# Second attention layer, groups 2 to 6: the query projection by seven block products (Strassen-Winograd) in place of eight

## The chip, the cores and the metric

One core of one Trainium2 chip. The metric is the device time of one execution in microseconds (us), lower is better. PE is TensorE, DVE VectorE, ACT ScalarE, POOL GpSimd, SP SyncE.

## What is computed

`x` has 16 sequences of 64 tokens, so T = 1024 tokens of E = 512. Two layers follow each other, each an attention block and a feed-forward block, each added to `x` behind a layer norm with a gate. The change is in the second layer's attention: H = 32 query heads of D = 128 and 8 key heads, so that 4 query heads share a key head; queries and keys are normed (rms) over D.

```
q = _rmsnorm((h @ Wq.T) as 32 heads of 128, q_norm_w)      # h = layernorm(x), 1024 x 512
k = _rmsnorm((ctx @ Wk.T) as 8 heads, k_norm_w), repeated for the 4 query heads of a group
scores = q . k / sqrt(128) + mask ; probs = softmax(scores)
x = x + tanh(g_xattn[1]) * ((probs . v) as 1024 x 4096) @ Wo.T
```

## The kernel before, in words

Every engine has its own instruction stream, written out by hand; semaphores join them. The order on each engine is that of the code. Activations stand transposed in SBUF, `hT` as 4 blocks of 128 rows (E) by 1024 tokens. Each fp32 operand is kept as a high part rounded to `fp32r` and a low part (the difference), `hT_hi` and `hT_lo`, `wq_hi` and `wq_lo`; a product is three matmuls, high with high, low with high, high with low (`three`, L226 to L228). ACT makes each high part by a copy, POOL each low part by a subtraction (`wq_lo`, L743; `wo_lo`, L1310).

An attention layer goes over G = 8 groups g of J = 4 heads and two halves h of 512 tokens; u = 2g + h is a unit. A step (g, h) of PE holds, in this order: the scores of unit u-1 (16 matmuls, L978), its folded sums of squares (L953, or L963 in the first units), the values of unit u-2 (24 matmuls, L1005), the query projection of unit u (4 heads of 12 matmuls 128x128 by 512 tokens), and the output projection of unit u-2 (4 token tiles of 12 such matmuls, into `ps_b`). In the steps (0, *) and (1, *), which open the layer, heads of the projection and the other pieces stand in a slightly different order: in (1,0) three heads, then the values of unit 0, then the fourth head.

ACT squares a head's queries into `q_sq` and copies them to `qT`; both read the PSUM bank in which PE has put the head. There are two such banks, used in turn, so the projection of head 2 waits for ACT's copy of head 0, and head 3 for head 1. DVE adds rows 0 to 63 and 64 to 127 of the squares to each other (`fold_squares`, L1470), and the scores of the unit wait for the last of these folds (`q_fold`). DVE transposes the sums of squares to `r_t` (semaphore `ssq_t`, for which the next projection waits) and copies them in eight 32x16 pieces to `r_s` (L1457); ACT makes 1/rms of them (`r_q`). DVE transposes the scores out of PSUM (L1435), scales them by `r_q` (L1479), adds the mask (L791), takes maxima (L1490, L1485), POOL or DVE subtracts them (`att_shift`, L797), ACT takes the exponential (L1177), DVE sums (L1502), POOL divides (`att_normalise`, L803), DVE transposes to `pT` (L1512), ACT makes `p_hi` (L1184) and DVE `p_lo` (L808), for which the values wait. Of their result in PSUM ACT makes `o_hi` and DVE `o_lo` (L1518), for which the output projection waits; DVE adds its tiles to `x_sb` (L1529).

In the layer's opening ACT's `r_q` of unit u-1 stands ahead of the squares and copies of heads of unit u. In the loop, POOL waits for DVE's `r_s` copies ahead of the second `wo_lo` of a step (g, 0):

```
for j in wo if do_finish and h == 0 and not (isinstance(g, int) and g == 1) else ():
    if lay and j == 1:
        pool.wait_ge(*c("ssq_all", us + 1))
    wo_low(g - 1, j)
```

The feed-forward block of this layer has small adapters; `lora_center` (L2132) is POOL's one part of it within the attention. It is written in POOL's step (0,1), and its instruction, at 766.31, falls into PE's step (1,0).

## Time and profile before

| | us |
|---|---|
| median of 3 runs | 1179.5 (1179.32 to 1179.86) |
| profiled execution | 1179.01 |
| its span | 1177.1 |
| PE busy | 1169.5 (99% of the span) |
| DVE busy | 880.9 (75%) |
| POOL busy | 532.9 (45%) |
| ACT busy | 424.0 (36%) |

The span runs from the first to the last instruction that the profiler records; 1.9 us lie outside. The second attention layer lies between 746 and 1150 us, and the steps that the change calls woven, (2,0) to (6,1), between the starts of the scores at 814.01 and at 1074.74.

### The profile page before, as it was taken

Reading aid. Unit: us, or ns where it says so; the run is one execution under the profiler, and the core shown is the slowest. Engines: PE = TensorE matmul, PEld = TensorE weight load, DVE = VectorE, ACT = ScalarE, POOL = GpSimd, SP = SyncE. Lnnn points to the kernel's source line nnn. Section 1 sums busy time; section 2 is a strip of 40 time slices with the busy share of each in tenths; the row PEclk is TensorE's granted clock in tenths of the full one; section 3 lists DMA queues with packets and bytes.
Section 4 is the critical chain, followed back from the end, with each engine's and each line's share of the span. In section 5 each row is a group of like instructions: output and inputs, shape, how many; then the busy total and the mean of one; then the engine's idle time right before and its main releaser. Section 6 shows DMA issues by size and latency. Waiting matters only on the chain.

```text
span 1177.1 us, 17132 instructions
## 1 busy us (share of the span) xinstructions
PE 1169.5 (99%) x6272; PEld 946.7 (80%) x6272; DVE 880.9 (75%) x1538; ACT 424.0 (36%) x748; POOL 532.9 (45%) x371
## 2 busy tenths in 40 slices
PE   9999999999999999999999999999999999999998
PEld 8888888888788888777788888777777777777776
DVE  4656646898888888889984335798888887888695
ACT  5145152322322222231552123535453443435542
POOL 5522533766667676677463112305242433425410
PEclk9999999999999999999999999999999999999999
DMA  7944735812211221211210003121221221121101
GB/s 286 285 137 159 211 111 162 287 55 81 81 66 59 89 80 45 80 45 45 99 64 36 1 1 107 55 94 57 91 80 45 80 80 54 71 89 39 43 1 72
DMA packets 57315, 106.54 MB, mean 91 GB/s; under 512 B 3633, under 2 KB 36529, under 8 KB 51889
## 3 DMA queue, kind: packets, MB, share of 16 engines
q1 hardware_dynamic: 56736, 104.82, 26.0%
q0 software_dynamic: 384, 1.05, 0.2%
q8 instruction: 32, 0.52, 0.2%
q14 instruction: 19, 0.15, 0.0%
q10 hardware_dynamic: 144, 0.00, 0.0%
HBM read 78.59 MB, written 27.26 MB: 90 GB/s over the span
## 4 chain that ended last, share of the span: by engine, by line
PE 96%; DVE 2%; issue 0%; ACT 0%; DVEq 0%; POOL 0%; POOLq 0%
PE ps_q L226 14%; PE ps_b L226 14%; PE ps_b L228 14%; PE ps_b L227 14%; PE ps_q L227 13%; PE ps_q L228 13%; PE ps_s L978 5%; PE ps_b L1005 4%; PE ps_s L278 1%; PE ps_q L953 1%; PE ps_q L2152 1%; PE ps_b L479 1%; PE ps_s L1847 1%; PE ps_q L529 0%; PE ps_b L529 0%
## 5 line engine op out<-in xcount | busy, mean ns | idle before, releaser
L226 PE MATMUL ps_q<-hT_hi,wq_hi 128*128 128x512 f32 x512 | 203.2, 397 | 0.0
L227 PE MATMUL ps_q<-hT_lo,wq_hi 128*128 128x512 f32 x512 | 199.6, 390 | 0.0
L228 PE MATMUL ps_q<-hT_hi,wq_lo 128*128 128x512 f32 x512 | 199.2, 389 | 0.0
L226 PE MATMUL ps_b<-wo_hi,o_hi 128*128 128x512 f32 x440 | 171.6, 390 | 0.0
L227 PE MATMUL ps_b<-wo_lo,o_hi 128*128 128x512 f32 x440 | 171.2, 389 | 0.0
L228 PE MATMUL ps_b<-wo_hi,o_lo 128*128 128x512 f32 x440 | 171.2, 389 | 0.0
L743 POOL TENSOR_TENSOR wq_lo<-wq_raw,wq_hi 128x512 fp32r<-128x512 f32 x64 | 90.2, 1413 | 112.8 <-ACT wq_hi L737 112.8
L1317 POOL TENSOR_TENSOR qT<-q_t 128x512 f32<-128x512 f32 x64 | 89.8, 1405 | 66.3 <-DVE q_t L1430 60.8
L226 PEld LDWEIGHTS ps_q<-hT_hi,wq_hi 128*128 128x128 f32 x512 | 96.1, 188 | 24.3 <-issue 1.5
L228 PEld LDWEIGHTS ps_q<-hT_hi,wq_lo 128*128 128x128 f32 x512 | 96.1, 188 | 20.3
L227 PEld LDWEIGHTS ps_q<-hT_lo,wq_hi 128*128 128x128 f32 x512 | 96.2, 188 | 18.7
L1310 POOL TENSOR_TENSOR wo_lo<-wo_raw,wo_hi 128x512 fp32r<-128x512 f32 x56 | 83.5, 1507 | 56.4 <-ACT wo_hi L1142 38.3
L1184 ACT ACTIVATE p_hi<-pT 128x1024 fp32r<-128x1024 f32 x32 | 34.0, 1061 | 189.7 <-DVE pT L1512 189.7
L226 PEld LDWEIGHTS ps_b<-wo_hi,o_hi 128*128 128x128 f32 x440 | 82.6, 188 | 18.4 <-issue 1.4
L228 PEld LDWEIGHTS ps_b<-wo_hi,o_lo 128*128 128x128 f32 x440 | 82.6, 188 | 17.1
L227 PEld LDWEIGHTS ps_b<-wo_lo,o_hi 128*128 128x128 f32 x440 | 82.6, 188 | 17.1
L1529 DVE SCALAR_TENSOR_TENSOR x_sb<-ps_b,gates,x_sb 128x512 f32<-128x512 f32 x115 | 81.4, 722 | 18.0 <-PE ps_b L228 17.5
L803 POOL TENSOR_TENSOR p_sb<-p_sb,p_rec 128x1024 f32<-128x1024 f32 x29 | 55.7, 1920 | 83.8 <-DVE p_rec L1506 83.8
L1518 DVE TENSOR_TENSOR o_lo<-ps_b,o_hi 128x512 fp32r<-128x512 f32 x128 | 81.8, 682 | 12.6 <-ACT o_hi L1191 10.7
L1191 ACT ACTIVATE o_hi<-ps_b 128x512 fp32r<-128x512 f32 x128 | 66.5, 607 | 34.0 <-PE ps_b L1005 26.7
L1177 ACT ACTIVATE p_sb<-s_sb,zero_b 128x1024 f32<-128x1024 f32 x32 | 37.2, 1162 | 96.9 <-POOL s_sb L797 93.5
L797 POOL TENSOR_TENSOR s_sb<-s_sb,mx_c 128x1024 f32<-128x1024 f32 x28 | 53.8, 1921 | 32.1 <-DVE mx_c L1485 32.1
(301 smaller groups left out, 2498.0 us busy)
## 6 DMA issues: line engine op xcount, KB each, us to landing
wq_raw<-in_wq SPq DMA_DIRECT2D x16, 1024.0 KB, 4.8
wo_raw<-in_wo SPq DMA_DIRECT2D x16, 1024.0 KB, 4.8
kT<-kT_spill SPq DMA_DIRECT2D x32, 256.0 KB, 4.3
v_hi<-v_hi_spill SPq DMA_DIRECT2D x16, 512.0 KB, 3.7
v_lo<-v_lo_spill SPq DMA_DIRECT2D x16, 512.0 KB, 4.7
v_hi_spill<-vs_hi SPq DMA_DIRECT2D x12, 512.0 KB, 5.4
v_lo_spill<-vs_lo SPq DMA_DIRECT2D x12, 512.0 KB, 6.7
kw_raw<-in_wk SPq DMA_DIRECT2D x4, 1024.0 KB, 9.2
```

The source lines that it names most:

```text
L226: nc.tensor.matmul(dst, l_hi, r_hi, start=first, stop=False)
L227: nc.tensor.matmul(dst, l_hi, r_lo, start=False, stop=False)
L228: return nc.tensor.matmul(dst, l_lo, r_hi, start=False, stop=last)
L743: nc.gpsimd.tensor_tensor(wq_lo[:, :, j * D:(j + 1) * D], wq_raw[:, :, j * D:(j + 1) * D], wq_hi[:, :, j * D:(j + 1) * D].bitcast(F32), AL ...
L797: eng.tensor_tensor(sc, sc, wide(mx_c[:, :], QB), ALU.subtract).then_inc(c["s_shifted"], 1)
L803: eng.tensor_tensor(pr, pr, wide(p_rec[:, :], QB), ALU.mult).then_inc(c["p_normed"], 1)
L978: last = nc.tensor.matmul(ps_s[par * S:(par + 1) * S, t * JS:(t + 1) * JS], kT[:, h, b:b + S], qT[:, h, :, b:b + S], start=True, stop=True)
L1191: nc.scalar.activation(o_hi[:, 2 * half:2 * half + 2, :, par * S:(par + 1) * S], ps_b[n].rearrange("p (t j q) -> p t j q", t=2, j=J), ACT. ...
L1310: nc.gpsimd.tensor_tensor(lo, wo_raw[:, j, :], hi.bitcast(F32), ALU.subtract).then_inc(c["wo_lo"], 1)
L1317: nc.gpsimd.tensor_tensor(qT[:, h, j, :], q_t1[:, j % 2, :], q_t2[:, j % 2, :], ALU.add).then_inc(c["q_rot"], 1)
L1518: nc.vector.tensor_tensor(o_lo[part], ps_b[n].rearrange("p (t j q) -> p t j q", t=2, j=J), o_hi[part].bitcast(F32), ALU.subtract).then_inc ...
L1529: nc.vector.scalar_tensor_tensor(x_sb[:, i, :], out_bank(u, t)[:, :], gates[:, lay:lay + 1], x_sb[:, i, :], ALU.mult, ALU.add).then_inc(c[ ...
```

## The change

In the second layer's steps (2,0) to (6,1) the projection of one unit (512 rows of E by 4 heads of 128 by 512 tokens) is cut into 2 by 2 blocks in each of its three dimensions: rows of E (two of the four blocks of 128), heads (two of four, WD = 256 columns), tokens (QT = 256). Eight block products would be the plain form; Winograd's form of Strassen's algorithm takes seven, of sums of blocks, and adds the results up. Of one block product PE issues 12 matmuls 128x128 by 256 tokens (`product`), 84 in a unit in place of 48 by 512.

- Left operands: `wq_raw` blocks a11, a12, a22 and the sums s1 to s4. POOL makes the four sums (128x512) and all seven low parts once a group, ACT the seven high parts.
- Right operands: two token blocks of `hT` as they are, and the mixed sums t1 to t4 (128x1024, both halves at once) of `hT`'s high and low parts. They are made once: ten sums and four low parts on POOL, four high parts on ACT, in steps (0,1), (1,0) and (1,1), beside the first group's weight sums.
- Results: PSUM banks `ps_q` and `ps_h` collect products; ACT copies one part to `qT` and one to `q_sq`, DVE adds four times a bank and a part in SBUF (`joined`), POOL adds once (`c22_made`).
- In the woven steps ACT and not DVE copies the eight pieces to `r_s` (`sums_by_quadrant`), folds are two additions 64x1024 in place of four 64x512, and the wait for `ssq_all` ahead of the second `wo_lo` is not there.
- The weight of the query norm is no longer applied in the copy to `qT` but, times the key's, when keys are staged (`kT_st`). The layer's loop runs over g = 2 to 5, and g = 6 is written out.

On PE:

```diff
+        def woven(lay, g):
+            return lay == 1 and not (isinstance(g, int) and g in (0, 1, G - 1))
...
+        WOVEN_PARTS = ("a11", "s2", "s3", "a12", "a22", "s1", "s4")
...
+            def project_woven(g, h):
+                u = 2 * g + h
...
+                def product(bank, name, right, first, last_one=False):
+                    if h == 0:
+                        turn = 7 * (g - 2) + WOVEN_PARTS.index(name) + 1
+                        pe.wait_ge(*c("woven_hi", turn))
+                        pe.wait_ge(*c("woven_lo", turn))
...
+                    for q in range(2):
+                        for k in range(2):
+                            col = slice(q * D, (q + 1) * D)
+                            dst, closes = bank[:, q * QT:(q + 1) * QT], last_one and (q, k) == (1, 1)
+                            nc.tensor.matmul(dst, l_hi[:, k, col], r_hi[:, k, :], start=first and (q, k) == (0, 0), stop=False, skip_group_check=True)
+                            nc.tensor.matmul(dst, l_hi[:, k, col], r_lo[:, k, :], start=False, stop=False, skip_group_check=True)
+                            last = nc.tensor.matmul(dst, l_lo[:, k, col], r_hi[:, k, :], start=False, stop=closes, skip_group_check=True)
...
+                pe.wait_ge(*c("ssq_t", u))
+                if h == 0:
+                    pe.wait_ge(*c("t_hi", 4))
+                    pe.wait_ge(*c("t_lo", 4))
+                product(ps_q[0], "a11", tokens(0, 0), True).then_inc(c["product"], 1)
+                product(ps_q[1], "s2", mixed(t2_hi, t2_lo), True, True).then_inc(c["product"], 1)
+                pe.wait_ge(*c("s_turned", u))
+                product(ps_h[0], "s3", mixed(t3_hi, t3_lo), True).then_inc(c["product"], 1)
+                pe.wait_ge(*c("copied", 2 * n + 1))
+                product(ps_q[0], "a12", tokens(1, 0), False, True).then_inc(c["q_done"], 1)
+                product(ps_h[1], "s1", mixed(t1_hi, t1_lo), True).then_inc(c["q_done"], 1)
+                pe.wait_ge(*c("joined", 4 * n + 2))
+                product(ps_h[0], "a22", mixed(t4_hi, t4_lo), False, True).then_inc(c["q_done"], 1)
+                pe.wait_ge(*c("copied", 2 * n + 2))
+                product(ps_h[1], "s4", tokens(1, 1), False, True).then_inc(c["q_done"], 1)
```

On ACT: the woven step, and what is added to step (1,0):

```diff
+                sums_by_quadrant(us)
+                norms(us)
+                act.wait_ge(*c("product", 3 * n + 1))
...
+                nc.scalar.activation(qT[:, h, 0:2, late], heads(ps_q[0]), ACT.Copy).then_inc(c["copied"], 1)
+                out_high(up, 0)
+                out_high(up, 1)
+                if building:
+                    woven_high(act, g + 1, "a11")
+                out_high(up, 2)
+                out_high(up, 3)
+                if building:
+                    woven_high(act, g + 1, "s2")
+                act.wait_ge(*c("q_done", 4 * u + 1))
...
+                nc.scalar.activation(q_sq[:, 0:2, early], heads(ps_q[0]), ACT.Square).then_inc(c["q_sq"], 1)
+                nc.scalar.activation(qT[:, h, 0:2, early], heads(ps_q[0]), ACT.Copy).then_inc(c["q_rot"], J)
+                act.wait_ge(*c("q_done", 4 * u + 2))
+                nc.scalar.activation(q_sq[:, 2:4, late], heads(ps_h[1]), ACT.Copy).then_inc(c["copied"], 1)
+                if building:
+                    woven_high(act, g + 1, "s3")
+                exponentials(us)
+                act.wait_ge(*c("joined", 4 * n + 3))
+                square(slice(2, 4), early)
+                if building:
+                    woven_high(act, g + 1, "a12")
...
+                act.wait_ge(*c("joined", 4 * n + 4))
+                square(slice(0, 2), late)
+                act.wait_ge(*c("c22_made", n + 1))
+                square(slice(2, 4), late)
+                if building:
+                    woven_high(act, g + 1, "a22")
+                    woven_high(act, g + 1, "s1")
+                    woven_high(act, g + 1, "s4")
...
+                probs_high(us)
...
+                if second_opening(lay, g, h):
+                    mixed_high(t1_hi, t1_f, 3)
+                    mixed_high(t2_hi, t2_f, 8)
```

On POOL: the mixed sums, the woven step, steps (1,0) and (1,1), and the end of (0,1):

```diff
+            def mixed_first(f, t, l, r):
+                pool.wait_ge(*lns[2]("lo", NT))
+                nc.gpsimd.tensor_tensor(by_half(f), quarters(hT_hi, *l), quarters(hT_hi, *r), ALU.subtract).then_inc(c["t_f"], 1)
+                nc.gpsimd.tensor_tensor(by_half(t), quarters(hT_lo, *l), quarters(hT_lo, *r), ALU.subtract).then_inc(c["t_f"], 1)
+            def mixed_joined(f, t, turn):
+                pool.wait_ge(*c("t_f", turn - 1))
+                nc.gpsimd.tensor_tensor(f[:, :, :], f[:, :, :], t[:, :, :], ALU.add).then_inc(c["t_f"], 1)
+            def mixed_next(f, l, r, turn, before):
+                pool.wait_ge(*c("t_f", before))
+                nc.gpsimd.tensor_tensor(by_half(f), quarters(hT_hi, *l), by_half(r), ALU.subtract).then_inc(c["t_f"], 1)
+                pool.wait_ge(*c("t_f", turn - 1))
+                nc.gpsimd.tensor_tensor(by_half(f), by_half(f), quarters(hT_lo, *l), ALU.add).then_inc(c["t_f"], 1)
...
+            def woven_step(g, h, next_wq):
+                u = 2 * g + h
...
+                late = slice(QT, HALF)
+                if h == 0:
+                    for j in range(J):
+                        wo_low(g - 1, j)
+                elif building:
+                    woven_sum(pool, g + 1, "s2")
+                    woven_sum(pool, g + 1, "s3")
+                    woven_low(pool, g + 1, "a11")
+                att_shift(pool, lay, u - 1)
+                pool.wait_ge(*c("copied", 2 * n + 2))
+                pool.wait_ge(*c("joined", 4 * n + 2))
+                nc.gpsimd.tensor_tensor(qT[:, h, 2:4, late], qT[:, h, 2:4, late], q_sq[:, 2:4, late], ALU.add).then_inc(c["c22_made"], 1)
+                if h and building:
+                    woven_sum(pool, g + 1, "s4")
...
+                att_normalise(pool, lay, u - 1)
+                if h == 0 and not (isinstance(g, int) and g == G - 2):
+                    woven_sum_first(pool, g + 1)
+                elif building:
+                    for name in WOVEN_PARTS[1:]:
+                        woven_low(pool, g + 1, name)
...
             def step(g, h, do_project, do_score, do_finish, next_wq):
                 uq, us = 2 * g + h, 2 * g + h - 1
+                if woven(lay, g):
+                    woven_step(g, h, next_wq)
+                    return
+                if second_opening(lay, g, h):
+                    mixed_joined(t3_f, t3_t, 6)
+                    att_normalise(pool, lay, us)
+                    mixed_next(t2_f, (1, 1), t1_f, 8, 3)
+                    woven_sum_first(pool, 2)
+                    woven_sum(pool, 2, "s2")
+                    woven_sum(pool, 2, "s3")
+                    woven_sum(pool, 2, "s4")
+                    mixed_low(t1_lo, t1_hi, t1_f, 1)
+                    return
+                if builds_woven(lay, g, next_wq):
+                    mixed_next(t4_f, (1, 0), t2_f, 10, 8)
+                    att_shift(pool, lay, us)
+                    mixed_low(t2_lo, t2_hi, t2_f, 2)
+                    woven_low(pool, 2, "a11")
+                    woven_low(pool, 2, "s2")
+                    att_normalise(pool, lay, us)
+                    woven_low(pool, 2, "s3")
+                    woven_low(pool, 2, "a12")
+                    mixed_low(t3_lo, t3_hi, t3_f, 3)
+                    woven_low(pool, 2, "a22")
+                    woven_low(pool, 2, "s1")
+                    mixed_low(t4_lo, t4_hi, t4_f, 4)
+                    woven_low(pool, 2, "s4")
+                    return
...
                     lora_center(pool)
+                    mixed_first(t1_f, t1_t, (0, 1), (0, 0))
+                    mixed_joined(t1_f, t1_t, 3)
+                    mixed_first(t3_f, t3_t, (1, 1), (0, 1))
```

On DVE, the woven step:

```diff
+                turn_sums(us, 1 - h, True)
+                turn_scores(us, 1 - h)
+                scale_scores(us)
+                dve.wait_ge(*c("copied", 2 * n + 1))
+                dve.wait_ge(*c("product", 3 * n + 2))
+                joined(part_b, ps_q[1], part_b).then_inc(c["joined"], 1)
+                att_mask(dve, lay, us, 1 - h)
+                dve.wait_ge(*c("joined", 4 * n + 1))
+                dve.wait_ge(*c("product", 3 * n + 3))
+                joined(part_d, ps_h[0], part_b).then_inc(c["joined"], 1)
+                maxima(us)
+                out_low(up, 0)
+                out_low(up, 1)
+                dve.wait_ge(*c("q_done", 4 * u + 3))
+                joined(qT[:, h, 2:4, early], ps_h[0], part_b).then_inc(c["joined"], 1)
+                out_low(up, 2)
+                dve.wait_ge(*c("q_done", 4 * u + 4))
+                joined(part_b, ps_h[1], part_b).then_inc(c["joined"], 1)
+                out_low(up, 3)
+                sums(us)
+                add_output(up, h, 0)
+                fold_woven(u, 0)
+                turn_probs(us)
+                fold_woven(u, 1)
+                att_probs_low(dve, lay, us)
+                for t in range(1, PAIRS):
+                    add_output(up, h, t)
```

What stands in POOL's queue from the end of step (0,1) to the end of step (1,1), after the 128x272 addition of `lora_center`. Before (L803 `att_normalise`, L743 `wq_lo` of the next group, L797 `att_shift`):

```order
L743 TENSOR_TENSOR wq_lo<-wq_raw,wq_hi 128x4x128 x4
L2132 TENSOR_TENSOR a_raw<-a_raw,a_mean 128x272
L803 TENSOR_TENSOR p_sb<-p_sb,p_rec 128x1024
L743 TENSOR_TENSOR wq_lo<-wq_raw,wq_hi 128x4x128
L797 TENSOR_TENSOR s_sb<-s_sb,mx_c 128x1024
L743 TENSOR_TENSOR wq_lo<-wq_raw,wq_hi 128x4x128 x2
L803 TENSOR_TENSOR p_sb<-p_sb,p_rec 128x1024
```

And of the change (L1562 to L1573 the mixed sums, L918 `att_normalise`, L827 and L848 the weight sums):

```order
L2498 TENSOR_TENSOR a_raw<-a_raw,a_mean 128x272
L1562 TENSOR_TENSOR t_f<-hT_hi 128x1024
L1563 TENSOR_TENSOR t_t<-hT_lo 128x1024
L1567 TENSOR_TENSOR t_f<-t_f,t_t 128x1024
L1562 TENSOR_TENSOR t_f<-hT_hi 128x1024
L1563 TENSOR_TENSOR t_t<-hT_lo 128x1024
L1567 TENSOR_TENSOR t_f<-t_f,t_t 128x1024
L918 TENSOR_TENSOR p_sb<-p_sb,p_rec 128x1024
L1571 TENSOR_TENSOR t_f<-hT_hi,t_f 128x1024
L1573 TENSOR_TENSOR t_f<-t_f,hT_lo 128x1024
L827 TENSOR_TENSOR wq_raw<-wq_raw 128x2x256
L848 TENSOR_TENSOR s_f<-wq_raw 128x512
```

Six additions of 128x1024 now stand between `lora_center` and the division of unit 1, and two (t2) between that and the first weight sum; the rest of t2 to t4, the sums and the low parts follow in step (1,1).

ACT's queue at the end of step (1,0), of the change (L1342 the exponential of unit 1, L1419 the high parts of t1 and t2, L1349 `p_hi` of unit 1, L1325 and L1327 `r_q` of unit 2; before, `p_hi` followed the exponential at once):

```order
L1342 ACTIVATE p_sb<-s_sb,zero_b 128x1024
L1419 ACTIVATE t_hi<-t_f 128x1024 x2
L1349 ACTIVATE p_hi<-pT 128x1024
L1325 ACTIVATE r_q<-r_s,eps_rms 128x32
L1327 ACTIVATE r_q<-r_q,zero_b 128x32
```

`p_hi` of unit 1 now stands behind the high part of t2, which waits for POOL.

DVE's queue in a woven step (g, 0). Before:

```order
L1444 STREAM_TRANSPOSE r_t<-ps_q 128x256
L1445 STREAM_TRANSPOSE r_t<-ps_q 128x256
L1457 COPY r_s<-r_t 32x16 x8
L1435 STREAM_TRANSPOSE s_sb<-ps_s 128x1024
L1479 TENSOR_TENSOR s_sb<-s_sb,r_q 128x1024
L791 TENSOR_TENSOR s_sb<-s_sb,mask_sb 128x1024
L1490 TENSOR_REDUCE mx_a<-s_sb 128x32
L1485 TENSOR_TENSOR mx_c<-mx_a 32x32 x4
L1518 TENSOR_TENSOR o_lo<-ps_b,o_hi 128x8x64 x4
```

And of the change (L1868 `joined`, the bank first):

```order
L1765 STREAM_TRANSPOSE r_t<-ps_q 128x256
L1766 STREAM_TRANSPOSE r_t<-ps_q 128x256
L1756 STREAM_TRANSPOSE s_sb<-ps_s 128x1024
L1807 TENSOR_TENSOR s_sb<-s_sb,r_q 128x1024
L1868 TENSOR_TENSOR qT<-ps_q,qT 128x2x256
L906 TENSOR_TENSOR s_sb<-s_sb,mask_sb 128x1024
L1868 TENSOR_TENSOR qT<-ps_s,qT 128x2x256
L1818 TENSOR_REDUCE mx_a<-s_sb 128x32
L1813 TENSOR_TENSOR mx_c<-mx_a 32x32 x4
```

The eight copies are gone from DVE, and two additions out of PSUM (there called `ps_s`, the bank is that of `ps_h`) stand ahead of the maxima; the other two stand between the four `o_lo`.

## Rows read from the trace of the kernel before

**Rows 1.** The page: span, busy times, shares of the chain
```profile
span 1177.1 us, 17132 instructions
PE 1169.5 (99%) x6272; PEld 946.7 (80%) x6272; DVE 880.9 (75%) x1538; ACT 424.0 (36%) x748; POOL 532.9 (45%) x371
...
PE 96%; DVE 2%; issue 0%; ACT 0%; DVEq 0%; POOL 0%; POOLq 0%
```

**Rows 2.** Chain that ended last (start, length, what): scores of steps (1,1), (2,0), (7,0)
```profile
787.71 1.95 PE ps_s L978 x16
...
814.01 1.88 PE ps_s L978 x16
...
1074.74 1.88 PE ps_s L978 x16
```

**Rows 3.** Busy time by engine over the ten steps
```profile
core 0: us, PE busy (x) PEld busy (x) DVE busy (x) ACT busy (x) POOL busy (x), PEclk, DMA share, GB/s
814.00:1075.00 261.00, 261.00 (x1525) 206.90 (x1526) 214.71 (x381) 113.86 (x201) 99.53 (x60) 1.00 0.19 67
```

**Rows 4.** Timeline of PE: start, length, line, tiles; projection, then values
```profile
899.78 0.39 PE L226 MATMUL ps_q<-hT_hi,wq_hi 128*128 128x512 f32 x1
900.01 0.39 PE L227 MATMUL ps_q<-hT_lo,wq_hi 128*128 128x512 f32 x1
...
921.05 0.28 PE L1005 MATMUL ps_b<-p_hi,v_lo 64*128 64x256 f32 x2
921.16 0.28 PE L1005 MATMUL ps_b<-p_hi,v_hi 64*128 64x256 f32 x2
```

**Rows 5.** Timeline of PE's weight loads, adapters' projection
```profile
1152.35 1.86 PEld L2152 LDWEIGHTS ps_q<-a_raw,xT 128*128 128x128 f32 x16
```

**Rows 6.** Timeline of DVE and POOL around masks, idle and beside POOL
```profile
847.55 1.23 DVE L791 TENSOR_TENSOR s_sb<-s_sb,mask_sb 128x1024 f32<-128x1024 f32 x1
...
871.23 1.29 POOL L1310 TENSOR_TENSOR wo_lo<-wo_raw,wo_hi 128x512 fp32r<-128x512 f32 x1 [3.04 <-DVE r_s L1457]
873.71 2.20 DVE L791 TENSOR_TENSOR s_sb<-s_sb,mask_sb 128x1024 f32<-128x1024 f32 x1
872.48 4.60 POOL L1310 TENSOR_TENSOR wo_lo<-wo_raw,wo_hi 128x512 fp32r<-128x512 f32 x2
```

**Rows 7.** Groups of instructions of POOL, 128x1024; and one such by timeline
```profile
L803 POOL TENSOR_TENSOR p_sb<-p_sb,p_rec 128x1024 f32<-128x1024 f32 x29 | 55.7, 1920 | 83.8 <-DVE p_rec L1506 83.8
...
422.73 2.40 POOL L808 TENSOR_TENSOR p_lo<-pT,p_hi 128x1024 fp32r<-128x1024 f32 x1 [1.28 <-ACT p_hi L1184]
```

**Rows 8.** Timeline of DVE, POOL and PE, first half of step (1,0)
```profile
765.71 1.95 DVE L1457 COPY r_s<-r_t 32x16 f32<-32x16 f32 x8
766.26 0.17 DVE L1457 COPY r_s<-r_t 32x16 f32<-32x16 f32 x1
766.44 0.67 DVE L1457 COPY r_s<-r_t 32x16 f32<-32x16 f32 x1
766.31 0.77 POOL L2132 TENSOR_TENSOR a_raw<-a_raw,a_mean 128x272 f32<-128x272 f32 x1 [3.65 <-ACT a_mean L2127]
767.69 1.23 DVE L808 TENSOR_TENSOR p_lo<-pT,p_hi 128x1024 fp32r<-128x1024 f32 x1
771.44 1.22 DVE L791 TENSOR_TENSOR s_sb<-s_sb,mask_sb 128x1024 f32<-128x1024 f32 x1
771.52 0.38 PE L1005 MATMUL ps_b<-p_hi,v_hi 64*128 64x256 f32 x2
```

**Rows 9.** One line's instructions, DVE: o_lo, first input in PSUM
```profile
L1518 DVE TENSOR_TENSOR o_lo<-ps_b,o_hi x128: 628/680/694, 228.5 to 1148.0; 128x512 fp32r<-128x512 f32 x128
```

**Rows 10.** Timeline of DVE and ACT, end of step (1,0)
```profile
786.20 1.41 DVE L1470 TENSOR_TENSOR q_sq<-q_sq 64x512 f32<-64x512 f32 x2
786.20 1.06 ACT L1184 ACTIVATE p_hi<-pT 128x1024 fp32r<-128x1024 f32 x1 [7.21 <-DVE pT L1512]
```

**Rows 11.** Timeline of ACT, last step: sums of squares
```profile
1121.19 1.90 ACT L1171 ACTIVATE r_s<-r_t 32x16 f32<-32x16 f32 x8 [3.32 <-DVE r_t L1447]
```

More of the change, by code:

```diff
@@ L19 @@
 JS = J * S
+QT = HALF // 2
+WD = 2 * D
 SC = PAIRS * JS
@@ new lines, in woven_parts @@
+        def woven_parts(name):
+            rows, cols = {"a11": (0, 0), "a12": (1, 0), "s1": (0, 1), "a22": (1, 1)}.get(name, (0, 0))
+            own = (slice(None), slice(2 * rows, 2 * rows + 2), slice(cols * WD, (cols + 1) * WD))
+            if name == "s2":
+                return s2_f[:, :, :], s2_hi[:, :, :], s2_lo[:, :, :]
+            if name == "s3":
+                return s3_f[:, :, :], s3_hi[:, :, :], s3_lo[:, :, :]
+            if name == "s4":
+                return s4_f[:, :, :], s4_hi[:, :, :], s4_lo[:, :, :]
+            return wq_raw[own], wq_hi[own], wq_lo[own]
```

229 lines of the change are left out of this document (193 added, 36 removed).

## The prediction

> **What bounds the kernel now.** The page comes first: PE is busy for 99% of a span of 1177.1 us and has 96% of the chain that ended last [rows 1]. So matmul time that goes comes off the end, and any wait that reaches PE is added to it. Second the chain: the scores of steps (2,0) and (7,0) start at 814.01 and 1074.74 [rows 2], ten steps in 260.7 us, 26.07 each, with no wait between. Third, what the other engines could take there: over those ten steps DVE is busy for 214.7 us of 261, ACT for 113.9, POOL for 99.5 [rows 3]. DVE has 4.6 us a step left, part of it bound to waits; on POOL much is free. Last, the room in the opening: PE's scores of step (1,1) start at 787.71 [rows 2]; the fourth fold of unit 2, for which they wait, ends at 786.20 + 1.41 = 787.61 [rows 10]. There is none.
>
> **What PE saves.** Projection matmuls of 512 tokens follow each other at 900.01 - 899.78 = 0.227 us; those with 256 columns, which go in pairs of rows, at 921.16 - 921.05 = 0.11 to 0.12 a pair [rows 4], 0.12 over a longer stretch. 128-column weight loads, one for each matmul, run at 1.86/16 = 0.116 [rows 5], just under that. I take 0.12: a unit has 48 x 0.2267 = 10.88 before and 84 x 0.12 = 10.08 after, 0.80 less, and ten units 8.0 less. At 0.116 it would be 11.4, at 0.125, 3.8: bounds for the pace.
> The Trainium skill, page "TensorE: Matmul & The Clock Gate", section "Back-to-back issue gap", gives a sustained pace of 81 ns at N = 128 and 131 ns at N = 512. Taken as a line between them, 256 columns would cost 98 ns, three quarters of 512 and not half, and by the ratio 84 x 98 against 48 x 131 the unit's 10.88 would become 14.2, ten units 33 us more. The rows have 227 ns where the page has 131, so I keep the rows.
>
> **What DVE and POOL do to each other.** A mask addition takes 1.23 us with POOL idle, and 2.20 when POOL has two `wo_lo` in hand; those two take 4.60, while one alone takes 1.29 [rows 6]. Two of 1.29 and two DVE additions (scale and mask) of 1.2 make 5.0, about that stretch. So they take turns, whole instruction by whole instruction, and the turn passes after each. It holds for small copies too: in `r_s`, one copy takes 0.17, the next, issued while POOL's 0.77 us addition runs, 0.67, until that ends [rows 8]. DVE instructions with an input in PSUM are free of it: 128 `o_lo` take 628 to 694 ns, whatever POOL does [rows 9]. Where POOL has one instruction now and then this costs nothing. The change puts rows of them there.
> A POOL addition of 128x1024 takes 1.92 with a broadcast input and 2.40 with two full ones [rows 7]. The mixed sums have two full ones: 2.40; the other end is 1.92.
>
> **The opening, step by step.** I follow every instruction from its queue and its semaphores, with the durations above and the turns; this is called the walk below. Before: POOL's `lora_center` ends at 767.08, the eight `r_s` copies at 767.66, `p_lo` of unit 0 runs 767.69 to 768.9, the mask from 771.44, and PE's values of unit 0 start at 771.52 [rows 8]. After: behind `lora_center` six additions of 2.40 follow at once. The fifth copy is the one held until 767.1; the last three wait for one addition each and are through at 769.5, 771.9 and 774.3, `p_lo` waits for the fourth, starts at 776.65 and ends at 777.7 (1.23, less 0.15 that a waiting instruction gains on its start). Values start at 777.8: **+6.3**. Scale and mask get their turns at 780.0 and 783.4, `o_lo` behind them ends at 785.8, where PE without it is ready at 782.0: **+3.8**. The second pair of `o_lo` gives **+0.45**. The division of unit 1 then ends at 796.0, DVE's transposition at 797.3, and the two last folds wait for t2's additions (2.40 each): 801.8, the scores of (1,1) start **+4.5** late. ACT's high part of t2 waits for t2 as well, and `p_hi` of unit 1, which ran at 786.20 [rows 10], stands behind it: values of unit 1 **+1.1**, sums' transposition +0.4. In (1,1) the `r_s` copies of unit 2 take turns with the low part of t1 and t4's two additions (3 x 2.40), and ACT's `r_q`, queued ahead of the squares of unit 3, holds the bank that head 2 needs: **+4.75**. The folds of unit 3 stand behind the division and five low parts: **+4.4**. Sum 25.7; the same walk of the kernel before gives 1.3 too much at the scores of (1,1), leaving 24.4. Then the first woven product waits for the low part of t4, +1.6, and one output for `o_lo`, +0.3. **Opening: +26.3.** The mechanism is robust in sign, since there is no room at 787.71, not in size: with 1.92 us in place of 2.40 the walk gives 6.8 less.
>
> **The woven steps.** DVE loses eight copies (1.4 us), gets four joins, each like `o_lo` 0.68, 2.7 us, and its four folds become two (1.41 for two of 512 [rows 10], so 1.1 for each of 1024, 0.6 less in all): about +0.7 a unit. ACT gets the eight copies at 1.90/8 = 0.24 us [rows 11], about as many copies and squares as it had, and is half idle: nothing by itself, but `r_q` comes some 0.5 later. POOL gets per group four sums, seven low parts for four, two additions to part C22: 9 x 1.29 = 11.6 us in 52. It has the time. But six low parts in a row now stand where DVE has its second fold and `p_lo`, and four `wo_lo` without the wait that had kept them behind the `r_s` copies (the "3.04 <-DVE r_s" of [rows 6]) stand at scale and mask. The walk gives, once per group in (g,0): scores 0.2 late for the fold, the first product 0.8 for the transposed sums queued behind `p_lo`, the product with a22 0.4 for the join that is queued behind the mask, the output 0.4 for `o_lo`: 1.8 for each of the four groups 3 to 6, **+7.2**. If DVE's and POOL's instructions fall otherwise, it is between 0 and 12. Of the new waits, POOL's for `joined` ahead of the C22 addition has the division and the low parts of the next group behind it, but the subtraction of the maxima ahead of it ends later than the join does; PE's for ACT's two copies of products end two products before they are asked for. SP's load of the next `wq_raw` waits for the seventh low part, some 20 us before its first use. The weight's factor, the removed increments, the moved small DMA and the written-out loop pass cost nothing I can find: they take instructions from engines that wait, hidden behind PE.
>
> **Sum.** -8.0 + 26.3 + 7.2 = +25.5 on 1179.0, the profiled execution (its span plus 1.9), 1204.5; the median of the runs is 0.5 above it. The 2.40 is the upper of its two prices, so I go slightly under: **1204**.
>
> **Rivals.** *A, the above,* 0.58: 1204, of its own 1196 to 1211 (the 1.92, 1198, the woven bounds, and clock: where PE stands for 4 to 6 us its granted clock could fall for a time, which no stretch here shows). *B, small copies keep their turn,* 0.15: the eight `r_s` copies wait once, not each, as if the 0.67 had been the only one that is ever held. The walk without them gives +15.2: 1194. For it: only one copy is seen held. Against: there was only one POOL instruction to hold them. The Trainium skill, page "SBUF — State Buffer", section "SBUF: two separate sides", has the port pair of these two engines as an exclusive lock, which whoever starts first keeps for its whole instruction, and names fp32 copies from SBUF to SBUF among those that take it; by that rule B's 1194 falls to A's 1204, and the held copy agrees. *C, the opening costs half of that or less and the woven steps give back what PE saves,* 0.08: 1181.5 to 1188. *D, the change's aim, faster,* 0.14: POOL's and DVE's instructions hardly hold each other (the 2.20 is a slow mask for another reason, as when the POOL input is what counts). The walk with no turns at all leaves 3.9 of stalls (`p_hi` of unit 1 behind t2, t4's low part) against 8.0: 1175. It decides from the point where opening and woven steps together lose less than 5.6 us, a sixth of the 33.5 that I have. Against it are the copies' 0.67 and the 4.60. *No difference,* 0.03. *E, small matmuls cost more than half,* 0.02: if each took the 946.7/6272 = 0.151 us that a weight load lasts in the mean of the whole run [rows 1], a unit would have 84 x 0.151 = 12.7, 1.8 more than before, ten 18: 1204.5 + 8 + 18 = 1231, or 1197 were the rest free. The pace in [rows 4, 5] speaks against it. By the figures of the Trainium skill above it would be 1246.
>
> **Range and chances.** A measurement of this kernel tells 0.2%, 2.4 us, from no change. Slower A + B + C + E = 0.83, same 0.03, faster 0.14. The range 1184 to 1212 leaves out D, the same, most of E and a part of C and of A's upper end, 2 in 10. A clock drop, or B with 1.92, stays within.
>
> **What would show it.** In the profile after: `r_s` copies of unit 1 with a mean over 1 us from 765.7 on, idle PE before values at about 777.8, before `ps_b` output, scores of (1,1) near 802, of (2,0) at about 838; `joined` near 0.7 us; ten woven steps in 260.7 - 8 + 9 = 261 to 262 us; block products at 0.12 us. Wrong if copies are not stretched, if the mixed sums run well under 1.9 us, if 256-column matmuls keep another pace, or if ten woven steps show less than 254 or over 268 us.

## The result and the profile after

The changed kernel takes 1203.57 us (median of 6 runs, 1203.34 to 1203.84) against 1179.41 for the kernel before, measured beside it (6 runs, 1178.95 to 1179.86): ratio 1.0205, interval 1.0192 to 1.0218. It is slower by 24.2 us. The profiled execution took 1203.78.

The page of the changed kernel (span; busy times; shares of the chain that ended last), against [rows 1]:

```profile
span 1202.0 us, 18025 instructions
PE 1170.3 (97%) x6632; PEld 960.7 (80%) x6632; DVE 930.4 (77%) x1478; ACT 446.6 (37%) x837; POOL 649.7 (54%) x430
...
PE 22%; DVE 10%; issue 3%; POOL 0%; DVEq 0%; ACT 0%
```

The span grew by 24.9 us, and PE is busy for 0.8 us more, with less to do. Both halves of that need an explanation: idle time that was not there before, and work that ran slower. The share of PE in the chain fell from 96% to 22%; the listed shares no longer add up, so the end is followed here on PE itself.

PE's timeline, the instructions of the opening with an idle time before them, and the scores of (7,0); the rows with L1138 are the scores of (1,1), (2,0) and (7,0), against [rows 2]:

```profile
775.55 0.39 PE L1165 MATMUL ps_b<-p_hi,v_hi 64*128 64x256 f32 x2 [3.70 <-issue]
...
783.40 0.47 PE L252 MATMUL ps_b<-wo_hi,o_hi 128*128 128x512 f32 x1 [1.67 <-issue]
...
789.40 0.47 PE L252 MATMUL ps_b<-wo_hi,o_hi 128*128 128x512 f32 x1 [0.28 <-DVE o_lo L1846]
...
799.31 3.68 PE L1138 MATMUL ps_s<-qT,kT 128*64 128x256 f32 x16 [4.21 <-issue]
804.23 0.39 PE L1165 MATMUL ps_b<-p_hi,v_hi 64*128 64x256 f32 x2 [0.21 <-DVE x_sb L1857]
...
814.61 0.80 PE L252 MATMUL ps_q<-hT_hi,wq_hi 128*128 128x512 f32 x1 [3.02 <-ACT qT L1318]
...
835.88 3.68 PE L1138 MATMUL ps_s<-qT,kT 128*64 128x256 f32 x16 [3.27 <-DVE q_sq L1791]
...
1097.86 1.95 PE L1138 MATMUL ps_s<-qT,kT 128*64 128x256 f32 x16
```

The scores of (1,1) come 11.6 us later than before and those of (2,0) 21.9. From (2,0) on little is added: (7,0) starts 262.0 us behind it, where ten steps took 260.7, and its values then wait 1.5. So nearly all of the loss arises in (1,0) and (1,1), as forecast. The two stretches of 16 scores at 3.68 us in place of 1.95 and 1.88 are the slower work.

Up to (2,0) there are seven idle times, 16.4 us in all, at places that the walk named; before, the same steps had 0.7, ahead of the scores of (1,1). What stands on the other side is in the timelines of DVE and POOL, first half of (1,0), against [rows 8], and in two rows of DVE from (1,1): the `r_s` copies of unit 2 and the last two folds of unit 3.

```profile
765.87 6.29 DVE L1778 COPY r_s<-r_t 32x16 f32<-32x16 f32 x8
772.19 3.26 DVE L923 TENSOR_TENSOR p_lo<-pT,p_hi 128x1024 fp32r<-128x1024 f32 x1
...
778.81 3.29 DVE L906 TENSOR_TENSOR s_sb<-s_sb,mask_sb 128x1024 f32<-128x1024 f32 x1
...
804.94 7.94 DVE L1778 COPY r_s<-r_t 32x16 f32<-32x16 f32 x8
...
831.13 4.52 DVE L1791 TENSOR_TENSOR q_sq<-q_sq 64x512 f32<-64x512 f32 x2
...
767.20 2.39 POOL L1562 TENSOR_TENSOR t_f<-hT_hi 128x1024 f32<-128x1024 f32 x1
...
772.02 2.34 POOL L1567 TENSOR_TENSOR t_f<-t_f,t_t 128x1024 f32<-128x1024 f32 x1
774.33 3.36 POOL L1562 TENSOR_TENSOR t_f<-hT_hi 128x1024 f32<-128x1024 f32 x1
```

Eight copies take 6.29 us in place of 1.95, `p_lo` 3.26 in place of 1.23, and the fourth POOL addition 3.36 in place of 2.39: each waits for the other engine's instruction in hand. In (1,1) the eight copies of unit 2 take 7.94, and the two folds that the scores of (2,0) wait for 4.52, where two took 1.41 [rows 10].

The slower work shows in windows. The columns are those of [rows 3]; the third number from the right is the granted clock as a share of 2.4 GHz:

```profile
775.50:789.00 13.50, 11.78 (x60) 9.28 (x60) 13.15 (x15) 5.35 (x8) 8.74 (x3) 0.87 0.00 1
799.30:803.00 3.70, 3.69 (x24) 2.00 (x32) 2.20 (x2) 1.40 (x2) 3.54 (x3) 0.50 0.02 4
...
815.00:820.00 5.00, 5.00 (x18) 3.96 (x18) 4.83 (x9) 2.48 (x6) 1.11 (x1) 0.75 0.00 0
836.00:840.00 4.00, 4.00 (x32) 1.82 (x32) 3.17 (x3) 0.00 (x0) 4.00 (x3) 0.50 0.00 0
840.00:845.00 5.00, 5.00 (x60) 4.34 (x45) 2.65 (x4) 3.12 (x12) 5.00 (x5) 0.86 0.23 66
845.00:1097.00 252.00, 245.05 (x1803) 211.14 (x1802) 231.25 (x313) 126.55 (x267) 162.76 (x97) 1.00 0.20 72
```

Each of the four idle times of 3.0 to 4.2 us lies in or ahead of such a stretch; 0.50 is the lower level, 1.2 GHz, for the whole of it. Length times what is missing from 1.00 is 1.76 + 1.85 + 1.25 + 2.00 + 0.70 = 7.6 us in the first five rows, some 8 with the stretches between them. The account at the scores of (2,1), 23.6 late (863.7 for 840.1), agrees: 0.3 by which the scores of (1,0) were late already, 15.7 of idle time more than before (16.4 less 0.7), less the 0.8 that the first woven unit saves, leave 8.4 for the clock by difference.

### The profile page after: what moved, and what is told of

The parts are those of the page before. It is cut to its first block and busy times, and to the rows that moved or that the text cites. A ratio compares the mean times of both kernels' runs of the same rounds, so it can differ in the third digit from the quotient of the medians.

```text
span 1202.0 us, 18025 instructions
## 1 busy us (share of the span) xinstructions
PE 1170.3 (97%) x6632; PEld 960.7 (80%) x6632; DVE 930.4 (77%) x1478; ACT 446.6 (37%) x837; POOL 649.7 (54%) x430
## 5 line engine op out<-in xcount | busy, mean ns | idle before, releaser
L252 PE MATMUL ps_q<-hT_hi,wq_hi 128*128 128x512 f32 x352 | 141.2, 401 | 3.0 <-ACT qT L1318 3.0
L253 PE MATMUL ps_q<-hT_lo,wq_hi 128*128 128x512 f32 x352 | 138.2, 393 | 0.0
L254 PE MATMUL ps_q<-hT_hi,wq_lo 128*128 128x512 f32 x352 | 137.8, 392 | 0.0
L1349 ACT ACTIVATE p_hi<-pT 128x1024 fp32r<-128x1024 f32 x32 | 33.9, 1061 | 171.7 <-DVE pT L1840 171.7
L918 POOL TENSOR_TENSOR p_sb<-p_sb,p_rec 128x1024 f32<-128x1024 f32 x29 | 55.6, 1918 | 62.8 <-DVE p_rec L1834 62.8
L252 PEld LDWEIGHTS ps_q<-hT_hi,wq_hi 128*128 128x128 f32 x352 | 66.7, 190 | 21.0 <-ACT qT L1318 3.4
L1342 ACT ACTIVATE p_sb<-s_sb,zero_b 128x1024 f32<-128x1024 f32 x32 | 37.0, 1156 | 120.1 <-POOL s_sb L912 113.7
L254 PEld LDWEIGHTS ps_q<-hT_hi,wq_lo 128*128 128x128 f32 x352 | 66.7, 189 | 14.4
L253 PEld LDWEIGHTS ps_q<-hT_lo,wq_hi 128*128 128x128 f32 x352 | 66.8, 190 | 12.9
L854 POOL TENSOR_TENSOR wq_lo<-wq_raw,wq_hi 128x512 fp32r<-128x512 f32 x44 | 66.1, 1511 | 18.7 <-ACT wq_hi L768 18.7
```

What stands on the lines that cost most here:

```text
L252: nc.tensor.matmul(dst, l_hi, r_hi, start=first, stop=False)
L253: nc.tensor.matmul(dst, l_hi, r_lo, start=False, stop=False)
L254: return nc.tensor.matmul(dst, l_lo, r_hi, start=False, stop=last)
L854: nc.gpsimd.tensor_tensor(wq_lo[:, :, j * D:(j + 1) * D], wq_raw[:, :, j * D:(j + 1) * D], wq_hi[:, :, j * D:(j + 1) * D].bitcast(F32), AL ...
L918: eng.tensor_tensor(pr, pr, wide(p_rec[:, :], QB), ALU.mult).then_inc(c["p_normed"], 1)
L1342: nc.scalar.activation(p_sb[:, :], s_sb[:, :], ACT.Exp, bias=zero_b[:, 0:1], scale=1.0 if lay else Q_SCALE).then_inc(c["p_exp"], 1)
```

## The experiments

The theory (A of the prediction): DVE and POOL take turns in the SBUF, whole instruction by whole instruction, and each idle time of PE also costs clock behind it. Its rivals: another part of the change makes the waits (the DVE joins, the removed wait, the moved copies), or the seven products themselves cost as much as eight.

**The long additions alone, in the kernel before.** Six additions of the size of the mixed sums, into a buffer that nobody reads there:

```diff
                     lora_center(pool)
+                    pool.wait_ge(*lns[2]("lo", NT))
+                    for n in range(6):
+                        if n:
+                            pool.wait_ge(lora["beside"], n)
+                        nc.gpsimd.tensor_tensor(ln_buf[:, :, :], hT_hi[:, 0:2, 0:E].bitcast(F32), hT_hi[:, 2:4, 0:E].bitcast(F32), ALU.subtract).then_inc(lora["beside"], 1)
```

> The kernel before, and behind lora_center on POOL six additions of 128x1024 of which nothing is used. Theory (DVE instructions with SBUF operands and POOL's instructions take turns): each of the last r_s copies and p_lo of unit 0 is held for one addition of 2.4, values of unit 0 start 4 to 6.5 late, the output projection another 1.5 to 4: 1185 to 1190. Rival (the delay comes from the order of the queues, p_hi behind the high part of t2, the division behind the sums): nothing here waits for the additions, 1179.4 within 0.5.

Measured: 1187.59, ratio 1.0073 (1.0057 to 1.009). The timeline of DVE, POOL and PE:

```profile
765.59 6.22 DVE L1462 COPY r_s<-r_t 32x16 f32<-32x16 f32 x8
766.92 17.46 POOL L1355 TENSOR_TENSOR ln_buf<-hT_hi 128x1024 f32<-128x1024 f32 x6
...
773.17 0.39 PE L1005 MATMUL ps_b<-p_hi,v_hi 64*128 64x256 f32 x2 [1.69 <-issue]
781.02 0.76 PE L226 MATMUL ps_b<-wo_hi,o_hi 128*128 128x512 f32 x1 [3.22 <-issue]
```

and the window behind the second wait:

```profile
781.00:785.00 4.00, 3.98 (x10) 3.13 (x11) 3.92 (x5) 0.00 (x0) 3.30 (x2) 0.50 0.00 0
```

The additions alone, with nothing else of the change, give the stretched copies, two new idle times on PE and the half clock behind the longer one. The wait ahead of the scores of (1,1) also grows, from 0.7 to 1.3. That is 8.4 us (1179.15 for the kernel before, measured beside it) out of six additions that no engine waits for: 5.5 of idle time more than before, and some 2.8 of clock.

**The same with memsets**, which write but read nothing (the edit against the run above):

```diff
-                        nc.gpsimd.tensor_tensor(ln_buf[:, :, :], ..., ALU.subtract).then_inc(lora["beside"], 1)
+                        nc.gpsimd.memset(ln_buf[:, :, :], 0.0).then_inc(lora["beside"], 1)
```

> The kernel before with six POOL instructions behind lora_center that write 128x1024 zeros and read nothing. Theory of turns for every POOL instruction: values of unit 0 late as with the additions, 1183 to 1188 if one takes 1 to 2.4 us. Rival (only POOL instructions that read SBUF hold DVE): 1178.9 to 1179.9.

Measured: 1180.80, ratio 1.0011 (1.0 to 1.0021), between the two ranges, so neither theory fits as it stands. The timeline says why:

```profile
766.11 5.33 DVE L1462 COPY r_s<-r_t 32x16 f32<-32x16 f32 x8
771.47 1.23 DVE L808 TENSOR_TENSOR p_lo<-pT,p_hi 128x1024 fp32r<-128x1024 f32 x1
...
767.42 6.02 POOL L1355 MEMSET ln_buf<- 128x1024 f32 x6
```

A memset takes 0.95 us. The copies are held by it (5.33 us for eight), but `p_lo`, with two inputs from the SBUF, runs its free 1.23 from 771.47 on while the last two memsets run beside it, at 771.47 for 0.95 and at 772.48 for 0.96, not held either. With the additions `p_lo` had 1.23 too, but the addition issued with it took 3.47, since it waited for `p_lo`. So what holds depends on both instructions: a copy waits for a POOL operation that reads and for one that only writes, and between an operation of two inputs and a memset there was no wait in the one place where they met. The Trainium skill, page "SBUF — State Buffer", section "SBUF: two separate sides", lists just these two cases for the shared pair of ports; the rows agree with it.

**The mixed sums at 16 columns**, in the changed kernel (1024 before), everything else in place:

```diff
+            tiny = lambda out, l, r, op: nc.gpsimd.tensor_tensor(out[:, 0, 0, 0:16], l[:, 0, 0, 0:16], r[:, 0, 0, 0:16], op)
-                nc.gpsimd.tensor_tensor(by_half(f), quarters(hT_hi, *l), quarters(hT_hi, *r), ALU.subtract).then_inc(c["t_f"], 1)
+                tiny(by_half(f), quarters(hT_hi, *l), quarters(hT_hi, *r), ALU.subtract).then_inc(c["t_f"], 1)
...
-                nc.scalar.activation(hi[:, :, :], f[:, :, :], ACT.Copy).then_inc(c["t_hi"], 1)
+                nc.scalar.activation(hi[:, 0, 0:16], f[:, 0, 0:16], ACT.Copy).then_inc(c["t_hi"], 1)
```

> The changed kernel with every mixed sum, its high and its low part cut to 16 columns; the products read hT in their place, so the second layer's values are others. Every wait and every place in a queue stays. Theory: the opening's stalls and the half clock behind them go almost all, 1181 to 1185 (1179.4 plus 1.3 of the woven steps, 1.8 of step (7,0) and what the weight sums and lows leave in (1,1)). Rival (the waits among the queues and not the length of POOL's work): still over 1195.

Measured: 1182.94, ratio 1.0032 (1.0021 to 1.0044), clock 1.00 throughout. So 20.6 of the 24.2 us hang on these sums and their parts, and the clock's loss goes with them. What is left is 1.8 ahead of the scores of (1,1), 1.0 in smaller waits, and mainly this, in the view of PE's waits (line waited for: us in all, times, longest):

```profile
PE ps_b L1165 <- DVE x_sb L1858: 8.6, 6, 1.7
```

**The weights' sums and lows small as well**, for groups 3 to 6:

```diff
+        def few(gt, t):
+            return t if isinstance(gt, int) and gt == 2 else t[:, 0:1, 0:16]
...
-                nc.gpsimd.tensor_tensor(lo, f, hi.bitcast(F32), ALU.subtract).then_inc(c["woven_lo"], 1)
+                nc.gpsimd.tensor_tensor(few(gt, lo), few(gt, f), few(gt, hi).bitcast(F32), ALU.subtract).then_inc(c["woven_lo"], 1)
```

> The run with cut mixed sums, and POOL's weight sums and low parts of groups 3 to 6 cut to 16 columns as well, with the high parts of the sums s2 to s4 on ACT (values of the second layer are others). Theory (what PE saves is 8.0, and the rest is what POOL's work does to DVE): the waits of the values in (g,0), 1.65 a group and 1.8 in step (7,0), go too, 1171.5 to 1175. Rival (the waits in the woven steps come from DVE's joins and the order of its queue, not from POOL): 1180 to 1183.

Measured: 1175.70, ratio 0.9966 (0.9952 to 0.9979), 0.7 above what was expected. Its waits, and its chain over the woven steps:

```profile
PE ps_b L1171 <- DVE x_sb L1864: 2.5, 2, 1.4
PE ps_s L1144 <- issue: 1.8, 1, 1.8
```

```profile
842.49 1.88 PE ps_s L1144 x16
...
1044.72 1.88 PE ps_s L1144 x16
```

Eight steps in 202.2 us, 25.28 each, against 26.07 in [rows 2]: PE does save 0.79 us a unit, with all of its matmuls in place. The rival that the seven products cost as much as eight is out, and so is the one that the DVE joins make the waits of the woven steps: all joins are in place here. Two waits in (1,1), 2.9 us, and one at the values of (7,0), 1.4, remain; what makes them was not taken apart.

**Shorter pieces.** Each mixed operation cut into four of 256 columns, so that DVE waits for less at a time:

```diff
+            def in_pieces(out, l, r, op):
+                for k in range(2):
+                    for hh in range(2):
+                        last = nc.gpsimd.tensor_tensor(out[:, k, hh, :], l[:, k, hh, :], r[:, k, hh, :], op)
+                return last
...
```

> The changed kernel with each mixed sum and low part of 128x1024 in four instructions of 128x256, same result. Theory (the turn passes after every instruction): a DVE instruction waits for at most 0.7 instead of 2.4, and the opening's 21.9 falls to 8 to 13, in spite of some 6 us more POOL time: 1190 to 1196. Rival (POOL keeps the turn over its row of instructions, or the total of POOL's work counts): 1203 to 1210.

Measured: 1202.83, ratio 1.0209 (1.0191 to 1.0227). It gains nothing, and my expectation missed. POOL's groups in (1,0) (the mean ns of one behind the comma):

```profile
L1563 POOL TENSOR_TENSOR t_t<-hT_lo 128x256 f32<-128x256 f32 x8 | 9.5, 1213 | 0.0
L1563 POOL TENSOR_TENSOR t_f<-t_f,t_t 128x256 f32<-128x256 f32 x8 | 6.5, 838 | 0.2
L1563 POOL TENSOR_TENSOR t_f<-hT_hi 128x256 f32<-128x256 f32 x8 | 5.6, 735 | 0.0
```

and ACT's second high part in its timeline:

```profile
799.15 1.06 ACT L1419 ACTIVATE t_hi<-t_f 128x1024 fp32r<-128x1024 f32 x1 [13.53 <-POOL t_f L1563]
```

A free quarter is 0.73 us; the groups' means are up to 1.21, DVE's turns included. Three operations in four pieces take 4 x (0.735 + 1.213 + 0.838) = 11.1 us in the mean of t1 and t3, where the whole ones took 7.1 for t1 and 10.0 for t3, 8.5 in the mean. Each hold is shorter, and there are more of them. PE's idle time in the opening is 16.4 us as before, at other places. The 3.70 ahead of the values of unit 0 is gone and the scores of (1,1) wait 1.32, but the values behind them wait 5.91, since the high part of unit 1's probabilities stands on ACT behind that of t2, and the first woven product waits 2.65 for the last low part of the mixed sums.

**The `r_s` copies of units 1 and 2 on ACT, and unit 1's high part ahead of t2's:**

```diff
+                    if isinstance(us, int) and us in (1, 2):
+                        sums_by_quadrant(us)
                     norms(us)
...
                     mixed_high(t1_hi, t1_f, 3)
+                    probs_high(us)
                     mixed_high(t2_hi, t2_f, 8)
+                    return
...
```

> The changed kernel; the eight r_s copies of units 1 and 2 are made by ACT, and p_hi of unit 1 stands ahead of the high part of t2. Theory (each copy on DVE loses turns to the mixed sums, three of 2.3 in unit 1 and three in unit 2): the values of unit 0 start 3 to 5 sooner, head 2 of unit 3 no longer waits its 3.0, the folds are held as before: 1194 to 1199. Rival (the holds only move to the next DVE instructions, p_lo, scale and mask): 1202 to 1204.

Measured: 1198.03, ratio 1.0159 (1.0145 to 1.0172), inside what was expected, 5.5 under the changed kernel. The way to it is in part the rival's, in the timeline of DVE and PE:

```profile
766.08 1.23 DVE L923 TENSOR_TENSOR p_lo<-pT,p_hi 128x1024 fp32r<-128x1024 f32 x1 [0.53 <-ACT p_hi L1351]
...
777.06 7.10 DVE L1819 TENSOR_TENSOR mx_c<-mx_a 32x32 f32<-32x32 f32 x4
...
788.34 0.76 PE L252 MATMUL ps_b<-wo_hi,o_hi 128*128 128x512 f32 x1 [6.62 <-DVE o_lo L1852]
```

`p_lo` now runs free, ahead of POOL's row, and the first wait of the values is gone. But POOL's six additions are still to come, and they hold what stands next: four `mx_c`, 0.77 us together in the changed kernel, take 7.10, and the output, which was 1.67 late, is 6.62 late. Unit 3's head 2 no longer waits its 3.02, and the scores of (1,1) wait 1.56 in place of 4.21. Taking the small copies away from DVE saves a part and moves another part of the turns to the next instructions.

**All of it together** (pieces, copies on ACT, high part first, and the additions of the section below):

> Both edits together, and the mixed sums in pieces of 128x256. Theory: with p_hi of unit 1 no longer behind t2, the 6.3 us wait of the run with pieces alone goes, and the pieces show their worth: 1188 to 1194. Rival (pieces are worth nothing since POOL's total time sets the end of the opening): 1191 to 1197, not under the sum of the two edits alone.

Measured: 1201.55, ratio 1.0186 (1.0172 to 1.02), and missed: worse than the copies and the high part alone. PE now waits longest at the scores of (2,0), for the folds of unit 3, in its timeline:

```profile
829.68 3.58 PE L1138 MATMUL ps_s<-qT,kT 128*64 128x256 f32 x16 [6.15 <-DVE q_sq L1804]
```

**The six low parts behind DVE's `p_lo`**, in the woven steps:

```diff
+                    pool.wait_ge(*c("p_lo", u))
                     for name in WOVEN_PARTS[1:]:
                         woven_low(pool, g + 1, name)
```

> The changed kernel with the six low parts of the next group behind p_lo of the same step. Theory: the second fold and p_lo are no longer held, the additions of the output behind them end in time and the values of steps (3,0) to (6,0) no longer wait their 1.6 to 1.7, that of (7,0) not touched: 1203.6 minus 5.5 to 7.5, 1196 to 1198. Rival (the values wait for the end of the output projection itself): 1203 to 1204; and if the low parts now come late for the products, above 1204.

Measured: 1212.71, ratio 1.0284 (1.0267 to 1.0301): 9.1 us above the changed kernel, where I expected a gain. PE's waits over the woven steps, of the changed kernel:

```profile
PE ps_b L1165 <- DVE x_sb L1857: 6.2, 4, 1.7
```

of this one:

```profile
PE ps_b L252 <- DVE o_lo L1847: 9.8, 4, 2.5
```

its timeline of POOL and PE behind (3,0)'s scores:

```profile
897.25 6.00 POOL L1547 TENSOR_TENSOR wo_lo<-wo_raw,wo_hi 128x512 fp32r<-128x512 f32 x4
...
905.17 0.77 PE L252 MATMUL ps_b<-wo_hi,o_hi 128*128 128x512 f32 x1 [2.52 <-DVE o_lo L1847]
```

and its window behind the wait:

```profile
905.00:907.00 2.00, 1.83 (x4) 1.49 (x5) 2.00 (x4) 1.48 (x2) 1.74 (x2) 0.50 0.86 365
```

The wait of the values is gone. In its place the low parts and `wo_lo` slide later into the next step, up to the maxima: four `mx_c` take 3.36 us there, 0.77 in the changed kernel, while scale and mask take what they took. The output waits 2.5 us, and behind that PE runs at 0.50. Idle time over the woven steps grows by 2.9 us; the rest of the 9.1 goes with the clock, 0.97 in the mean of 863 to 1110 for 1.00 in the changed kernel. The same work of POOL costs more or less by what of DVE stands beside it.

**Output additions 1 and 2 ahead of the folds** on DVE:

```diff
                 add_output(up, h, 0)
+                add_output(up, h, 1)
                 fold_woven(u, 0)
                 turn_probs(us)
+                add_output(up, h, 2)
                 fold_woven(u, 1)
                 att_probs_low(dve, lay, us)
-                for t in range(1, PAIRS):
-                    add_output(up, h, t)
+                add_output(up, h, 3)
```

> The changed kernel; in DVE's woven step the additions of output tiles 1 and 2 stand ahead of the first and the second fold, where the queue waits for POOL anyway, and no longer behind p_lo. Theory (values of the (g,0) steps wait for these additions, which stand behind a fold and p_lo held by POOL's low parts): two additions of 0.67 less in the wait, 1.2 to 1.4 in each of four groups and in step (7,0): 1197 to 1199. Rival (the values wait for the end of the output projection or for p_lo itself): 1203 to 1204.

Measured: 1205.40, ratio 1.0216 (1.0202 to 1.023), missed. Its waits over the woven steps:

```profile
PE ps_s L1138 <- DVE q_sq L1799: 6.8, 7, 1.5
...
PE ps_b L1165 <- DVE x_sb L1857: 1.1, 4, 0.4
```

and the timeline of DVE and POOL at the end of (2,1), with the second fold, for which the scores of (3,0) wait:

```profile
889.96 1.67 DVE L1799 TENSOR_TENSOR q_sq<-q_sq 64x1024 f32<-64x1024 f32 x1
...
889.27 5.72 POOL L820 TENSOR_TENSOR wq_lo<-wq_raw,wq_hi 128x512 fp32r<-128x512 f32 x3
```

The values' wait falls from 6.2 to 1.1, and the scores' rises from 0.7 to 6.8. The first fold comes to its turn 0.01 us after a low part of POOL has taken it (885.77 against 885.76) and takes 2.38; the second comes behind another addition of the output and is held by the next low part. It ends at 891.6, and the scores have waited 1.48.

**Two parts of the change tested by themselves.** The wait for the squares that had stood ahead of the second `wo_lo` put back into the woven steps, and in the kernel before the `r_s` copies of (2,0) to (6,1) given to ACT:

```diff
                     for j in range(J):
+                        if j == 1:
+                            pool.wait_ge(*c("ssq_all", u))
                         wo_low(g - 1, j)
```

> The changed kernel with the wait for the sums of squares ahead of the second wo_lo put back in the woven steps. Theory: the r_s copies are now ACT's, so the wait guards nothing, and wo_lo already starts when they are nearly done: 1203 to 1204.5. Rival (taking the wait away cost something, scale and mask being held by the third and fourth wo_lo): 1198 to 1202.

```diff
                 if do_score and lay:
+                    if wide_steps(g):
+                        last_sums(us)
                     norms(us)
...
```

> The kernel before with one part of the change alone: in steps (2,0) to (6,1) ACT and not DVE makes the eight r_s copies. Theory (no wait reaches PE in these steps, and ACT is half idle): 1178.9 to 1180. Rival (ACT's copies make r_q later and hold the squares and copies for which the projection of head 2 waits): 1181 to 1186.

Measured: 1203.46, ratio 1.0203 (1.0189 to 1.0217), and 1178.96, ratio 0.9997 (0.9988 to 1.0006). Neither does anything, as both expectations had it.

## Why the forecast of 1204 held, and where its steps did not

**What PE saves: right.** 0.80 a unit was forecast, 0.79 was measured with the waits gone. With the mixed sums at 20.6 us and the weights' parts at 1182.94 - 1175.70 = 7.2, 4.2 is left over 1179.4 - 7.9, and the sum is -7.9 + 20.6 + 7.2 + 4.2 = +24.1, the 24.2 to rounding. It closes by construction, since the 4.2 is a remainder; but PE's waits that are left there, 1.8 + 2.5, come to the same. The arithmetic saved is real; four times as much, 32 us, is lost to waits and clock that the count of matmuls does not mention.

**The turns of DVE and POOL: right,** the stretched copies included, so rival B falls. D falls with the six additions in the kernel before, C with the 15.7 us of idle time in the opening, more than half of 26.3 before any clock, and E with the pace of the products. The six additions show 8.4 us of the mixed sums' 20.6 by themselves; that the rest comes from the same turns is read from the timelines.

**The opening's idle times: the places right, the sizes too large.** The walk had 24.4 us at the scores of (2,0) over the kernel before; 15.7 us of idle time over it was measured. At the values of unit 0 it had +6.3, and they came at 775.55, 4.0 after 771.52. The step that failed is "the last three wait for one addition each". Three of the eight copies were held in all, for 0.66, 2.34 and 2.34 us, and of the last three one got through between two additions. That is one turn of 2.4 us less, and what follows came earlier with it: `o_lo` by some 2.5 us, so 1.67 idle and not 3.8. Later terms: scores of (1,1) 4.21 for 4.5, unit 3's head 2 3.02 for 4.75, scores of (2,0) 3.27 for 4.4, values of unit 1 0.21 for 1.1. Three small terms did not show as idle time: the sums' transposition (0.4), the first woven product behind t4's low part (1.6) and one output (0.3). The low part ended at 841.29 (838.95 + 2.34 in POOL's timeline), and PE, slowed by its clock, came to that product at 842.54; in the run with pieces, whose low parts take longer, the wait is there.

**The clock: a term that was left out of the sum.** The prediction had it as something that could happen after 4 to 6 us of idle time, inside the range. It happened after every idle time of 3.0 us and more, and cost some 8 us. The two errors, 24.4 against 15.7 and 0 against 8, cancel, and that was luck. The 1204 is therefore better than its working: 1203.6 without the clock's 8.4 would have been 1195, just outside the 1196 to 1211 that the prediction gave its own theory.

**The woven steps: the size right, the place wrong.** The forecast was -8.0 + 7.2, plus 1.6 for t4's low part and 0.3 for an output; ten steps took 1.3 us more than before. Besides the 2.7 us of clock left over in (2,0), the waits are 6.2 + 0.7, about what the +7.2 said. The values of (7,0) wait 1.5 more, for which the sum had no term. But the product, the join and `o_lo` that were to be late were not: four times the values wait, because the addition to `x_sb` that frees their bank is queued behind the folds and `p_lo`, all held. The timeline of DVE in the changed kernel, around the scores of (3,0) at 889.20:

```profile
883.01 2.48 DVE L1799 TENSOR_TENSOR q_sq<-q_sq 64x1024 f32<-64x1024 f32 x1
...
886.67 2.30 DVE L1799 TENSOR_TENSOR q_sq<-q_sq 64x1024 f32<-64x1024 f32 x1
889.00 2.19 DVE L923 TENSOR_TENSOR p_lo<-pT,p_hi 128x1024 fp32r<-128x1024 f32 x1
891.12 2.06 DVE L1857 SCALAR_TENSOR_TENSOR x_sb<-ps_b,gates,x_sb 128x512 f32<-128x512 f32 x3
```

Two folds (free: 1.2), `p_lo` (1.23), then the additions. The joins ran at 0.68 us as forecast.

**Costed at nothing, and rightly:** the removed wait and ACT's copies, by the last two runs. The weight's factor, the moved DMA and the written-out pass had no run of their own; with POOL's work cut, everything but the saving came to 4.2 us in all.

That the half clock is caused by the idle time, and not only follows it, rests on its coming and going together in several kernels; no run changed the clock alone. Whether the change can win at all is open too: with the full computation every rearrangement tried stayed at 1198 or above. Making the mixed sums on another engine than POOL, or starting the woven steps a group later, was not tried.

## What to carry to other kernels

Before giving work to an engine that looks free, ask which engine it shares the SBUF with: POOL was idle for over half of the time, and 28 us of what it was given came out at PE, because DVE had no slack at the instructions beside it. Shorter pieces gained nothing, and another order moved most of the holds to the next instruction (5.5 us saved at best); only less work on POOL (16 columns in place of 1024) took them away. And where PE stands still for 3 us, count the slower matmuls behind it as well: here half as much again as the idle time itself.
